# Attention on one core: one packing layout for all heads, odd heads scoring in the array's upper rows, and dense matmuls at the first exps

## The chip, the core and the metric

The kernel runs on one core of a Trainium2 chip. The metric is the device time of the program in microseconds (us). The engines are TensorE (PE; PEld is its weight load), VectorE (DVE), ScalarE (ACT), GpSimd (POOL) and SyncE (SP), which here only issues DMAs. Each has its own instruction queue and runs in order; semaphores join them.

## The reference

The input is x of 1024 tokens by 256 features. It passes through four residual blocks, each behind a layer norm:

```
x = x + attn_a(layernorm(x))     # 16 heads of 16, full softmax over 1024 keys, LoRA on Wq, Wk, Wv, Wo
x = x + ffn(layernorm(x))        # 256 -> 1024, exact gelu, -> 256; both weights ternary
x = x + attn_b(layernorm(x))     # 16 heads of 48 = q, k, v of 16; mixes heads of one token
x = x + ffn(layernorm(x))
```

The change touches `attn_a` alone: per head `softmax(q k^T / 4) v` with 1024 queries and 1024 keys.

## The kernel before

**Setup (0 to about 30 us).** x is normalised and transposed, the LoRA products are merged into the weights, and q and k are projected in eight items (`ITEMS`: q or k, heads 0 to 7 or 8 to 15, first or second half of the tokens). Each projection is cut into an fp16 first part (ACT, `first_part`) and a rest (DVE, `second_part`). A head's q and k then take 64 partition rows: four terms of 16, so that one fp16 matmul over 64 rows gives nearly an fp32 product. Two spare rows of the 64 carry the softmax shift.

**Where the terms lie.** For heads 0 to 7 all four terms are written out (`first_halves`, in the memory of `pbuf`, ACT writing one part twice). For heads 8 to 15 only three are (`last_halves`, in `parts`).

**Packing.** DMAs issued by SP (eight also by POOL) spread a head's terms from 16 partitions to the 64 rows of `k_rows` and `q_rows` (`spread`). For heads 0 to 7 that is one DMA a call, for 8 to 15 two. The upper 64 partitions get the queries again, and, in a separate tensor `k_far` in `parts`, the second half of the keys (`whole_group` repeats them by two DMAs a group). There are four groups of four heads.

**Maximum pass.** A tile of 128 queries against 1024 keys is two matmuls, one in the lower 64 rows (near keys) and one in the upper 64 (far keys), into a pair of PSUM banks (`max_tile`). DVE reduces 1024 columns to the row maximum (`take_max`, L1097). Sixteen tiles make a unit; a unit is a group of four heads and half of the queries, eight units in all (u = 0 to 7). When the sixteen are there, DVE cuts the maxima in two fp16 parts (`cut_max`), PE transposes them (`shift_rows`), ACT copies them to `m_rows`, and SP writes them by a DMA into the spare rows of the queries (`land_shift`).

**Score, exp and PV.** A unit has 32 steps. Step s takes head s % 4 and 128 keys: one score matmul of 64 rows (L1405) into one of three banks, one exp on ACT (L888) into `pbuf`; every fourth step PE multiplies four tiles by v (`times_v`, L1419, fp32, four column groups of 32). In the same loop every second step has a maximum tile of the next unit, and at the end of a unit's steps those of the unit after it begin, so the first seven (`LEAD`) of a unit stand ahead. Before the scores of a unit PE waits for its shift to have landed (`shift_landed`). At the end of a unit ACT copies PV out to `o_un` (`evacuate_pv`, L873), which lies in `parts` too. Unit 7 runs in the tail, whose order on all engines is the hand-written list `TAIL_ORDER`.

**Order on SP around the change.** Groups 0 and 1 are packed early. Then, in the order of the program: shift of unit 0; the 24 spreads and two repeats of group 2; two bias loads; shift of unit 1; the 24 spreads and two repeats of group 3; shift of unit 2; then the later shifts, one a unit. SP stops at each wait, and what stands behind it waits with it.

**Before the loop.** PE does the sixteen maximum tiles of unit 0 with the last two q items and the eight v projections between them, then the seven lead tiles of unit 1, behind the first of which stand the merged Wo (`merged_weight`) and the transposition of unit 0's maxima. At the fourth lead tile it waits for the first shift, and then starts the scores. `keep_clock` issues dense 128x128x512 matmuls; before, only at the start of the program (17).

Of the kernel before, what the change touches and what calls it, by code (L numbers as in the profile page):

```python
# [50 lines left out]
SHIFT_ROWS = (slice(59, 64, 4), slice(61, 64, 2))  # L51
# [21 lines left out]
WARM_UP = 17  # L73
SCORE_BANKS = (4, 5, 7)
# [213 lines left out]
def build(nc, a):  # L288
# [6 lines left out]
    with ExitStack() as ctx:  # L295
# [17 lines left out]
        last_halves = parts[:, 2048:8192].bitcast(F16).rearrange("p (m a t) -> p m a t", m=2, a=TWO + 1)  # L313
        k_far = parts[:, 8192:16384].bitcast(F16).rearrange("p (h t) -> p h t", h=H)
# [6 lines left out]
        far_group = parts[:, 8192:16384].bitcast(F16).rearrange("p (g j t) -> p g j t", g=NG, j=G)  # L321
# [117 lines left out]
        far_keys_packed = sem("far_keys_packed")  # L439
# [70 lines left out]
        def term(c, m, which, v):  # L510

            if c == 0:
                return first_halves[:, m, (0, 1 if m == K_ else 2, 3)[which], v]
            return last_halves[:, m, which, v]

        def first_terms(c, m, v):

            if c == 0:
                return first_halves[:, m, 0:3:2, v] if m == K_ else first_halves[:, m, 0:2, v]
            return last_halves[:, m, 0:1, v]  # L520

        def spread(eng, rows, m, h, v, done):

            c, hh = divmod(h, HC)
            src = slice(HD * hh, HD * hh + HD)
            if c == 0:
                eng.dma_start(rows, first_halves[src, m, :, v]).then_inc(done, 16)
                return
            for i in range(TWO):
                if i == 0:  # L530
                    terms = last_halves[src, m, 0:2, v] if m == K_ else \
                        last_halves[src, m, 0:1, v].broadcast_to([HD, TWO, v.stop - v.start])
                else:
                    terms = last_halves[src, m, 0:3:2, v] if m == K_ else last_halves[src, m, 1:3, v]
                eng.dma_start(rows[ROWS // 2 * i:ROWS // 2 * i + ROWS // 2], terms).then_inc(done, 16)  # L535

        def near_keys(eng, h, v, done):
            spread(eng, k_rows[0:ROWS, h, v], K_, h, v, done)

        def far_keys(eng, h, done):  # L540
            spread(eng, k_far[ROWS:2 * ROWS, h, :], K_, h, slice(HALF, T), done)
# [5 lines left out]
        def group_count(g):  # L547
            return 16 * 3 * G * (1 if g < NG // 2 else TWO)
# [12 lines left out]
        def _(sp):  # L561
# [30 lines left out]
            for j in range(G):  # L592
                near_keys(sp, j, first_half, head_packed[j])
            part_is_cut(sp, K_, 0, 1)
            for j in range(G):
                far_keys(sp, j, head_packed[j])
# [5 lines left out]
            for j in range(G):  # L602
                near_keys(sp, j, second_half, far_keys_packed)
# [3 lines left out]
            def whole_group(g):  # L607
                for h in range(G * g, G * g + G):
                    near_keys(sp, h, whole, group_packed[g])
                    for qh in (0, 1):  # L610
                        queries(sp, h, 0, qh, group_packed[g])
                sp.wait_ge(group_packed[g], group_count(g))
                sp.dma_start(k_far[ROWS:2 * ROWS, G * g:G * g + G, :], k_rows[0:ROWS, G * g:G * g + G, HALF:T]) \
                    .then_inc(group_repeated[g], 16)
# [3 lines left out]
            whole_group(1)  # L618

            def land_shift(g, qh, u):  # L620
# [3 lines left out]
                else:  # L624
# [4 lines left out]
                sp.dma_start(q_rows[SHIFT_ROWS[g // 2], g, qh, :, :].rearrange("o h t -> o (h t)"),  # L629
                             m_rows[0:TWO * n, :]).then_inc(shift_landed, 16)  # L630
# [4 lines left out]
            whole_group(2)  # L635
# [4 lines left out]
            whole_group(3)  # L640
# [124 lines left out]
        def _(act):  # L765
# [39 lines left out]
            def first_part(i):  # L805
# [3 lines left out]
                src = is_filled(act, ("proj", i)).unsqueeze(1).broadcast_to([P, TWO if c == 0 else 1, HALF])  # L809
# [80 lines left out]
            def exp_unit(g, qh, u):  # L890
# [16 lines left out]
            for done in (far_keys_packed, second_half_packed):  # L907
                act.wait_ge(done, 16 * G)
            act.wait_ge(group_packed[1], group_count(1))
            for s in range(G):  # L910
                exp_tile(0, s)
            with act.Fori(0, NG - 1) as g:
                exp_unit(g, 0, g * 2)
                exp_unit(g, 1, g * 2 + 1)

                for n in (2, 3):
                    act.wait_ge(group_packed[n], group_count(n))
# [361 lines left out]
        def _(pe):  # L1279
# [82 lines left out]
            def keep_clock(n):  # L1362
                for _ in range(n):
                    pe.matmul(ps[:, PAIR_BANKS[0], :], onesb[:, 0:P], onesb[:, :], start=True, stop=True)  # L1364

            pe.wait_ge(consts, 4)
            keep_clock(WARM_UP)
# [3 lines left out]
            def max_tile(g, qh, u, k):  # L1371
# [8 lines left out]
                for n, keys in ((0, k_group[0:ROWS, at, j, 0:HALF]), (1, far_group[ROWS:2 * ROWS, at, j, :])):  # L1380
                    q = q_rows[ROWS * n:ROWS * n + ROWS, at, qh, j, P * qt:P * qt + P]
                    ins = pe.matmul(ps[:, b + n, :], q.rearrange("p g t -> p (g t)"), keys.rearrange("p g t -> p (g t)"),  # L1382
                                    start=True, stop=True)
# [14 lines left out]
            def score_tile(g, qh, u, s):  # L1398
# [6 lines left out]
                pe.matmul(ps[:, b, :], k_group[0:ROWS, at, j, P * c:P * c + P].rearrange("p g t -> p (g t)"),  # L1405
# [238 lines left out]
```

## Time and profile before

| | |
|---|---|
| three runs | 352.35, 353.03, 353.84 us; median 353.03 |
| the profiled execution | 353.56 us; span of its instructions 351.7 us, so 1.86 us lie around it |
| busy share of the span | PE 92%, DVE 80%, ACT 69%, POOL 37% |
| chain that ended last | PE 63%, SP's queue 10%, DVE 8%, ACT 7%, POOL 5%, issue 3%, DMA 2% |
| granted TensorE clock, mean | 0.976 of full |

The page cuts the span into 40 slices of 8.8 us and gives busy tenths:

```profile
PE   7999786999979999999999999999998978779796
PEld 3653342222212222222222244338744735447685
DVE  7466999799978999999999543516959997999774
ACT  1575113688858888988888867896479533577694
```

The chain of waits goes back from the last instruction to what released each; the timeline gives instructions in order of time, merged where they follow each other; the idle time before one stands in brackets with the instruction or DMA that ended it. Matmul ends are modelled: a 512-column matmul is recorded with some 0.38 us, while the next one on the same rows starts some 0.22 us after it.

### The profile page before, as it was taken

How to read it: one execution, taken by the hardware profiler on the slowest of the kernel's cores; microseconds unless marked ns; L12 is line 12 of the kernel's file. 1: busy time of each engine (PE TensorE's matmuls, PEld its weight loads, DVE VectorE, ACT ScalarE, POOL GpSimd, SP SyncE). 2: the span in 40 equal slices, each digit the busy share in tenths (PEclk: the TensorE clock that was granted, in tenths of full speed). 3: DMA queues.
4: the chain of work that ended last, by engine and by line, in shares of the span. 5: the costliest groups of instructions: out<-in, count | busy, mean ns of one | idle time of the engine just before them, and what ended most of it. 6: DMA issues, size and time to landing. Idle time of an engine off the chain costs nothing.

```text
span 351.7 us, 5515 instructions
## 1 busy us (share of the span) xinstructions
PE 324.5 (92%) x1909; PEld 146.1 (42%) x1909; DVE 280.6 (80%) x471; ACT 243.5 (69%) x465; POOL 128.5 (37%) x133
## 2 busy tenths in 40 slices
PE   7999786999979999999999999999998978779796
PEld 3653342222212222222222244338744735447685
DVE  7466999799978999999999543516959997999774
ACT  1575113688858888988888867896479533577694
POOL 5042019999200000000006000400499959995030
PEclk9999998799989999999999999999999989999899
DMA  8937862354340000000000000000000000000011
GB/s 223 315 56 141 140 174 38 64 112 88 64 92 0 1 2 1 2 0 3 0 3 1 1 2 1 2 0 2 0 3 0 1 0 2 0 0 2 1 61 60
DMA packets 14814, 14.57 MB, mean 41 GB/s; under 512 B 4995, under 2 KB 13126, under 8 KB 14598
## 3 DMA queue, kind: packets, MB, share of 16 engines
q1 hardware_dynamic: 12358, 12.09, 15.1%
q10 hardware_dynamic: 2176, 1.64, 1.6%
q0 software_dynamic: 256, 0.52, 0.9%
q8 instruction: 15, 0.25, 0.3%
q14 instruction: 9, 0.07, 0.1%
HBM read 5.78 MB, written 1.05 MB: 19 GB/s over the span
## 4 chain that ended last, share of the span: by engine, by line
PE 63%; SPq 10%; DVE 8%; ACT 7%; POOL 5%; issue 3%; DMA 2%; ACTq 0%; DVEq 0%; POOLq 0%
PE ps L1419 14%; PE ps L1405 12%; SPq L535 8%; PE ps L1559 6%; PE ps L1547 6%; PE ps L1382 5%; PE ps L1334 4%; DVE mx L1097 3%; POOL pbuf L750 3%; PE ps L1532 3%; PE ps L1364 2%; PE ps L1591 2%; DMA pack<-m_rows 1%; ACT ps L931 1%; PE ps L1302 1%
## 5 line engine op out<-in xcount | busy, mean ns | idle before, releaser
L1097 DVE TENSOR_REDUCE mx<-ps 128x1 f32<-128x1024 f32 x128 | 150.3, 1219 | 9.8 <-PE ps L1382 8.6
L888 ACT ACTIVATE pbuf<-ps 128x512 f32<-128x512 f32 x256 | 135.7, 600 | 29.7 <-PE ps L1405 28.6
L1405 PE MATMUL ps<-pack 64*128 64x512 f16 x256 | 87.7, 386 | 3.6 <-DMA pack<-m_rows 1.9
L1419 PE MATMUL ps<-pbuf,v_slot 128*32 128x512 f32 x512 | 69.7, 618 | 1.1 <-ACT parts L873 1.1
L1405 PEld LDWEIGHTS ps<-pack 64*128 64x128 f16 x256 | 23.3, 95 | 82.1 <-ACT pbuf L888 48.5
L1382 PE MATMUL ps<-pack 64*128 64x512 f16 x128 | 49.2, 387 | 5.1 <-DVE mx L1097 4.8
L1382 PE MATMUL ps<-parts,pack 64*128 64x512 f16 x128 | 50.2, 399 | 0.0
L750 POOL TENSOR_TENSOR pbuf<-wT 128x1024 f32<-128x1024 f32 (+3 forms) x32 | 48.2, 1538 | 3.4 <-ACT wT L960 3.4
L705 POOL COPY v_slot<-v_sb 128x512 f32<-128x512 f32 x8 | 4.9, 614 | 113.5 <-PE ps L1419 92.0
L681 POOL TENSOR_TENSOR rstd<-rstd,minus_half 128x2 f32<-128x2 f32 x16 | 11.3, 708 | 71.7 <-DVE rstd L1016 71.7
L1191 DVE SCALAR_TENSOR_TENSOR pack<-ps,g_unit,pack 128x512 f16<-128x512 f32 (+1 forms) x40 | 24.6, 639 | 14.2 <-ACT pack L943 14.1
L1547 PE MATMUL ps<-v_sb,w_nat 128*128 128x512 f16 (+1 forms) x160 | 31.0, 337 | 2.7 <-DVE v_sb L1183 2.5
L1559 PE MATMUL ps<-w_nat,pack 128*128 128x256 bf16 x256 | 31.4, 273 | 0.8 <-DVE pack L1191 0.8
L931 ACT ACTIVATE ps<-ps,b_col 128x512 f32<-128x512 f32 (+1 forms) x40 | 23.5, 610 | 8.1 <-PE ps L1547 8.1
L1559 PEld LDWEIGHTS ps<-w_nat,pack 128*128 128x128 f16 x256 | 25.0, 98 | 5.4 <-DVE pack L1191 1.0
L1204 DVE TENSOR_REDUCE s_wide<-pbuf 128x64 f32<-128x1024 f32 (+3 forms) x32 | 25.4, 813 | 2.2 <-POOL pbuf L750 2.0
L943 ACT ACTIVATE pack<-ps,g_unit 128x512 f16<-128x512 f32 (+1 forms) x40 | 23.5, 643 | 0.2
L953 ACT ACTIVATE xn<-x_res,offset,rstd 128x256 f32<-128x256 f32 x24 | 13.1, 595 | 13.8 <-POOL offset L686 13.7
L1547 PEld LDWEIGHTS ps<-v_sb,w_nat 128*128 128x128 f16 x160 | 15.3, 99 | 15.6 <-DVE v_sb L1183 2.8
L1382 PEld LDWEIGHTS ps<-pack 64*128 64x128 f16 x128 | 11.9, 94 | 22.9 <-DVE mx L1097 12.3
L1419 PEld LDWEIGHTS ps<-pbuf,v_slot 128*32 128x32 f32 x512 | 10.4, 108 | 18.8 <-issue 18.1
L733 POOL TENSOR_TENSOR x_res<-x_res,w_nat 128x512 f32<-128x512 f32 x12 | 15.2, 1272 | 2.3 <-ACT xn L953 2.3
(145 smaller groups left out, 392.8 us busy)
## 6 DMA issues: line engine op xcount, KB each, us to landing
w_nat<-in_L_ffn_w_dram SPq DMA_DIRECT2D x2, 1024.0 KB, 6.7
pack<-pack SPq DMA_DIRECT2D x3, 512.0 KB, 4.9
pack<-pbuf SPq DMA_DIRECT2D x20, 64.0 KB, 2.5
x_res<-in_L_attn_a_x_dram SPq DMA_DIRECT2D x4, 256.0 KB, 3.6
pack<-parts SPq DMA_DIRECT2D x16, 64.0 KB, 2.3
pack<-parts SPq DMA_DIRECT2D x32, 32.0 KB, 2.0
out_dram<-x_res SPq DMA_DIRECT2D x4, 256.0 KB, 2.1
w_nat<-in_L_attn_b_Wqkv_dram ACTq DMA_DIRECT2D x1, 768.0 KB, 5.8
```

The source lines that it names most:

```text
L535: eng.dma_start(rows[ROWS // 2 * i:ROWS // 2 * i + ROWS // 2], terms).then_inc(done, 16)
L750: pool.tensor_tensor(out, in0, in1, ALU.mult).then_inc(products, 1)
L888: act.activation(pbuf[:, c % 2, j, :], ps[:, b, :], ACT.Exp, scale=scale_bits).then_inc(drained[b], 1)
L931: act.activation(src, src, ACT.Gelu, bias=b1_col[:, f:f + 1]).then_inc(gelu_ready, 1)
L1097: dve.tensor_reduce(mx[:, par, k:k + 1], ps[:, b:b + 2, :].rearrange("p b k -> p (b k)"), AX_X, ALU.max) \
L1191: dve.scalar_tensor_tensor(out=g_lo[:, kept(r, s), f, 0:width], in0=bank(key)[:, 0:width], scalar=g_unit[:, f:f + 1], in1=g_hi[:, kept(r, ...
L1204: dve.tensor_reduce(s_raw[:, t % 2, i, 0:nj], terms, AX_X, ALU.add).then_inc(reduced, 1)
L1382: ins = pe.matmul(ps[:, b + n, :], q.rearrange("p g t -> p (g t)"), keys.rearrange("p g t -> p (g t)"), start=True, stop=True)
L1405: pe.matmul(ps[:, b, :], k_group[0:ROWS, at, j, P * c:P * c + P].rearrange("p g t -> p (g t)"), q_rows[0:ROWS, at, qh, j, :].rearrange("p ...
L1419: ins = pe.matmul(ps[32 * j:32 * j + 32, PV_BANK, :], v_slot[:, qh, c, j, :], pbuf[:, c % 2, j, :], start=(c == 0), stop=(c == TT - 1))
L1547: ins = pe.matmul(out, w1T[:, c, P * f:P * f + P], x12[:, part, c, v], start=(part == 0 and c == 0), stop=(part == 1 and c == DC - 1))
L1559: ins = pe.matmul(out, part[:, k, f, v], w2T[:, f, :], start=(f == 0 and n == 0 and i == 0), stop=(f == FC - 1 and n == 1 and i == 1))
```

## The change

1. **One layout.** `last_halves` gets four terms like `first_halves`; ACT writes the first part twice for heads 8 to 15 too. `spread` is one DMA for every head. Group 1 takes 8 spreads in place of 12, groups 2 and 3 take 8 each in place of 24.
2. **Keys in both halves.** `k_far` goes; `k_rows` is filled in the upper 64 partitions too, with all 1024 keys. The repeat of a group's keys is 512 KB in place of 256 KB.
3. **Order on SP.** All spreads of groups 2 and 3 come first, then the repeats of 2, the repeats of 3, the bias loads, and then the shift of unit 1. ACT waits for both groups before the first PV copy.
4. **Odd heads.** `score_tile` uses the upper rows for heads 1 and 3 of a group. So the shift is written into both halves: two DMAs a unit.
5. **Dense matmuls.** Three ahead of each of the last two maximum tiles of unit 0, and three ahead of each of the seven lead tiles of unit 1: 27 in all, into the PV bank, the first three behind a wait for that bank's last v copy.

```diff
-        last_halves = parts[:, 2048:8192]...(m=2, a=TWO + 1)
-        k_far = parts[:, 8192:16384]...
+        last_halves = parts[:, 0:8192]...(m=2, a=TWO * TWO)
 def spread(eng, rows, m, h, v, done):
-            if c == 0:
-                eng.dma_start(rows, first_halves[src, m, :, v]).then_inc(done, 16)
-                return
-            for i in range(TWO):
...
-                eng.dma_start(rows[ROWS // 2 * i:ROWS // 2 * i + ROWS // 2], terms).then_inc(done, 16)
+            eng.dma_start(rows, (last_halves if c else first_halves)[HD * hh:HD * hh + HD, m, :, v]).then_inc(done, 16)
+        def both_queries(eng, h, done):
+            g, j = divmod(h, G)
+            spread(eng, q_rows[0:ROWS, g, :, j, :], Q_, h, slice(0, T), done)
 # SP, packing
-                near_keys(sp, j, second_half, far_keys_packed)
+                keys(sp, j, j % 2, second_half if j % 2 == 0 else first_half, score_keys_packed)
+            def spread_group(g):
+                for h in range(G * g, G * g + G):
+                    keys(sp, h, 0, whole, group_packed[g])
+                    both_queries(sp, h, group_packed[g])
+            def repeat_group(g):
+                sp.wait_ge(group_packed[g], GROUP_COUNT)
+                sp.dma_start(k_rows[ROWS:2 * ROWS, <group g>], k_rows[0:ROWS, <group g>]).then_inc(group_repeated[g], 16)
+                sp.dma_start(q_rows[ROWS:2 * ROWS, g], q_rows[0:ROWS, g]).then_inc(group_repeated[g], 16)
 # land_shift
-                sp.dma_start(q_rows[SHIFT_ROWS[g // 2], g, qh, :, :]..., m_rows[0:TWO * n, :])
+                for r in range(TWO):
+                    sp.dma_start(q_rows[slice(ROWS * r + 59, ROWS * r + 64, 4), g, qh, :, :]..., m_rows[0:TWO * n, :])
 # SP, order
             land_shift(0, 0, 0)
-            whole_group(2)
+            spread_group(2)
+            spread_group(3)
+            repeat_group(2)
+            repeat_group(3)
             (two bias loads)
             land_shift(0, 1, 1)
-            whole_group(3)
             land_shift(1, 0, 2)
 # ACT, first_part
-                src = ....broadcast_to([P, TWO if c == 0 else 1, HALF])
+                src = ....broadcast_to([P, TWO, HALF])
 # ACT, exp_unit
+                if qh == 0:
+                    for n in (2, 3):
+                        act.wait_ge(group_packed[n], GROUP_COUNT)
                 evacuate_pv(g, qh, u)
 # PE, score_tile
-                pe.matmul(ps[:, b, :], k_group[0:ROWS, ...], q_rows[0:ROWS, ...])
+                rows = slice(ROWS * (j % 2), ROWS * (j % 2) + ROWS)
+                pe.matmul(ps[:, b, :], k_group[rows, ...], q_rows[rows, ...])
 # PE, before the loop
             for k in range(FILLS):
+                if k >= FILLS - 2:
+                    pe.wait_ge(drained[PV_BANK], base[PV_BANK])
+                    keep_clock(KEEP_UP, PV_BANK)          # KEEP_UP = 3
                 max_tile(0, 0, 0, k)
             for k in range(LEAD):
+                keep_clock(KEEP_UP, PV_BANK)
                 max_tile(0, 1, 1, k)
```

## Rows read from the trace of the kernel before

**Rows 1.** Chain that ended last, stretch 97 to 104 (start, us, what)

```profile
97.98 4.39 DMA pack<-m_rows
103.61 1.86 PE ps L1419 x8
107.43 0.99 PE ps L1419 x8
```

**Rows 2.** Timeline of ACT: shift copy, PV copies, exps (start, us; idle in brackets)

```profile
75.22 0.27 ACT L869 COPY m_rows<-ps 128x128 f16<-128x128 f16 x1 [0.42 <-PE ps L1396]
...
83.54 0.58 ACT L873 COPY parts<-ps 128x512 f32 x1
106.55 0.58 ACT L873 COPY parts<-ps 128x512 f32 x1
126.35 0.58 ACT L873 COPY parts<-ps 128x512 f32 x1
146.06 0.58 ACT L873 COPY parts<-ps 128x512 f32 x1
...
199.78 2.06 ACT L888 ACTIVATE pbuf<-ps 128x512 f32<-128x512 f32 x4 [0.33 <-PE ps L1405]
```

**Rows 3.** Timeline of PE and its weight loads: shift waits, unit 6 without max passes

```profile
80.66 0.11 PEld L1405 LDWEIGHTS ps<-pack 64*128 64x128 f16 x2 [0.52 <-DMA pack<-m_rows]
...
102.42 0.39 PE L1405 MATMUL ps<-pack 64*128 64x512 f16 x1 [1.87 <-DMA pack<-m_rows]
...
199.36 0.82 PE L1405 MATMUL ps<-pack 64*128 64x512 f16 x3
200.43 0.39 PE L1405 MATMUL ps<-pack 64*128 64x512 f16 x1 [0.26 <-ACT pbuf L888]
```

**Rows 4.** Timeline of DVE, maxima of units 0 and 1

```profile
33.93 1.23 DVE L1097 TENSOR_REDUCE mx<-ps 128x1 f32<-128x1024 f32 x1 [0.62 <-PE ps L1382]
...
46.58 5.84 DVE L1097 TENSOR_REDUCE mx<-ps 128x1 f32<-128x1024 f32 x5 [0.28 <-PE ps L1382]
...
54.72 9.14 DVE L1097 TENSOR_REDUCE mx<-ps 128x1 f32<-128x1024 f32 x8 [0.54 <-PE ps L1382]
65.71 8.44 DVE L1097 TENSOR_REDUCE mx<-ps 128x1 f32<-128x1024 f32 x7 [1.85 <-PE ps L1382]
```

**Rows 5.** Windows: engines' busy us (instructions), granted clock, DMA share, GB/s

```profile
35.00:40.00 5.00, 3.83 (x18) 1.82 (x16) 4.96 (x7) 0.75 (x2) 0.00 (x0) 1.00 0.89 148
...
61.00:66.00 5.00, 5.00 (x22) 1.07 (x20) 3.15 (x4) 2.34 (x5) 4.67 (x4) 0.54 0.34 62
...
75.00:80.00 5.00, 5.00 (x33) 1.32 (x33) 5.00 (x5) 4.30 (x9) 4.72 (x4) 1.00 0.87 203
```

**Rows 6.** Timeline, all engines, 49 to 50: maximum tile 14, last v copy

```profile
49.64 0.39 PE L1382 MATMUL ps<-pack 64*128 64x512 f16 x1
49.74 0.37 ACT L816 COPY v_sb<-ps 128x256 f32<-128x256 f32 x1 [1.22 <-PE ps L1352]
```

**Rows 7.** Timeline of SP's queue, 34 to 98

```profile
34.09 8.22 SPq L527 DMA_DIRECT2D pack<-pbuf  x12
...
55.92 16.75 SPq L535 DMA_DIRECT2D pack<-parts  x24
...
78.27 0.73 SPq L629 DMA_DIRECT2D pack<-m_rows  x1
...
97.32 0.61 SPq L615 DMA_DIRECT2D pack<-pack  x1
```

**Rows 8.** Lines by form: first parts on ACT (busy, mean ns)

```profile
L810 ACT ACTIVATE pbuf<-ps,kq_scaled 128x1024 f16<-128x1024 f32 x4 | 4.5, 1116 | 1.3 <-PE ps L1334 1.2
L810 ACT ACTIVATE parts<-ps,kq_scaled 128x512 f16<-128x512 f32 x4 | 2.7, 684 | 2.7 <-PE ps L1334 2.7
```

**Rows 9.** Chain that ended last, stretch 206 to 236

```profile
208.43 0.54 PE ps L1405 x2
...
229.68 0.54 PE ps L1405 x2
```

More of the change, by code:

```diff
@@ L50 @@
 ROWS = TWO * TWO * HD
-SHIFT_ROWS = (slice(59, 64, 4), slice(61, 64, 2))
+SHIFT_ROWS = slice(59, 64, 4)
 DROPPED = HD - TWO
@@ L73 @@
 WARM_UP = 17
+KEEP_UP = 3
 SCORE_BANKS = (4, 5, 7)
@@ L628, in land_shift @@
                 n = G * TT // 2
-                sp.dma_start(q_rows[SHIFT_ROWS[g // 2], g, qh, :, :].rearrange("o h t -> o (h t)"),
-                             m_rows[0:TWO * n, :]).then_inc(shift_landed, 16)
+                for r in range(TWO):
+                    sp.dma_start(q_rows[slice(ROWS * r + SHIFT_ROWS.start, ROWS * r + SHIFT_ROWS.stop, SHIFT_ROWS.step), g, qh, :, :]
+                                 .rearrange("o h t -> o (h t)"), m_rows[0:TWO * n, :]).then_inc(shift_landed, 16)
             land_shift(0, 0, 0)
@@ L808, in first_part @@
                 out = first_terms(c, m, slice(HALF * s, HALF * s + HALF))
-                src = is_filled(act, ("proj", i)).unsqueeze(1).broadcast_to([P, TWO if c == 0 else 1, HALF])
+                src = is_filled(act, ("proj", i)).unsqueeze(1).broadcast_to([P, TWO, HALF])
                 act.activation(out, src, ACT.Identity,
@@ L906, in _ @@
                 act.wait_ge(head_packed_by_pool[j], 32)
-            for done in (far_keys_packed, second_half_packed):
+            for done in (score_keys_packed, second_half_packed):
                 act.wait_ge(done, 16 * G)
-            act.wait_ge(group_packed[1], group_count(1))
+            act.wait_ge(group_packed[1], GROUP_COUNT)
             for s in range(G):
@@ L1379, in max_tile @@
                     pe.wait_ge(drained[b], base[b] + u * (FILLS // 2) + k // 2)
-                for n, keys in ((0, k_group[0:ROWS, at, j, 0:HALF]), (1, far_group[ROWS:2 * ROWS, at, j, :])):
-                    q = q_rows[ROWS * n:ROWS * n + ROWS, at, qh, j, P * qt:P * qt + P]
-                    ins = pe.matmul(ps[:, b + n, :], q.rearrange("p g t -> p (g t)"), keys.rearrange("p g t -> p (g t)"),
+                for n in (0, 1):
+                    rows = slice(ROWS * n, ROWS * n + ROWS)
+                    ins = pe.matmul(ps[:, b + n, :], q_rows[rows, at, qh, j, P * qt:P * qt + P].rearrange("p g t -> p (g t)"),
+                                    k_group[rows, at, j, HALF * n:HALF * n + HALF].rearrange("p g t -> p (g t)"),
                                     start=True, stop=True)
@@ L1404, in score_tile @@
                 at = bass.ds(g, 1)
-                pe.matmul(ps[:, b, :], k_group[0:ROWS, at, j, P * c:P * c + P].rearrange("p g t -> p (g t)"),
-                          q_rows[0:ROWS, at, qh, j, :].rearrange("p g t -> p (g t)"), start=True, stop=True) \
+                rows = slice(ROWS * (j % 2), ROWS * (j % 2) + ROWS)
+                pe.matmul(ps[:, b, :], k_group[rows, at, j, P * c:P * c + P].rearrange("p g t -> p (g t)"),
+                          q_rows[rows, at, qh, j, :].rearrange("p g t -> p (g t)"), start=True, stop=True) \
                     .then_inc(filled[b], 1)
```

64 lines of the change are left out of this document (22 added, 42 removed).

## The prediction

> **What bounds the kernel now.** I read the page's chain of waits first: SP's queue holds 10% of it and a DMA 2%, although SP computes nothing. In order of time the chain runs from the first shift through SP's issues up to the DMA that writes the shift of unit 2: it is issued at 97.98 and lands 4.39 us later [rows 1]. PE stands 1.87 us before the scores of unit 2 [rows 3], and the next PV group takes 1.86 us in place of 0.99, for the clock has fallen [rows 1]. The PV copies on ACT price the whole: they lie 23.01 us apart over this unit (83.54 to 106.55), then 19.80 and 19.71 [rows 2]. One stall costs 3.3 us against 19.71.
>
> Then the other dip of the clock. From 61 to 66 the granted clock is 0.54, most of it at the lower of its two levels, 1.2 GHz [rows 5]. DVE, elsewhere without a pause, stands 1.85 us there waiting for a maximum tile [rows 4]. The cut of unit 1's maxima, behind the seven that end at 74.15, depends on that run.
>
> Third, the loop. A group of four steps takes 2.39 us (exps of unit 6 start at 199.78 and at 202.17, four exps 2.06 and 0.33 idle before them [rows 2]). I looked at unit 6 behind its last maximum tile, since there PE has only scores and PV: it idles 0.26 us for a bank that ACT must free, and the pace is the same [rows 3]. So the loop is a circle of latencies: last exp of four, score, PV, next score, its exp. PE's load is not what sets it. DVE is nearly as long: a maximum takes 1.14 to 1.21 us (9.14/8, 5.84/5, 8.44/7 [rows 4]; I use 1.18), and two fall in a group of four steps: 2.36.
>
> **The shift of unit 2 (gain).** With the spreads of group 3 moved ahead, SP has nothing but two small DMAs between the shift of unit 1 and that of unit 2, a unit later. The stall goes: 3.3 us [rows 2]. What is late next is the shift of unit 1.
>
> **The shift of unit 1 (cost).** Before, SP issued it at 78.27, behind 24 spreads (16.75 us, 0.70 each with the holds), two repeats and the biases [rows 7], and PE waited 0.52 us until 80.66 [rows 3], so it is wanted at 80.14. After:
> - The spreads began at 55.92 [rows 7]; now 1.1 later (see the dense matmuls) and one more DMA of the first shift, 0.7: 57.7.
> - 16 spreads x 0.70 = 11.2 us of issuing, to 68.9. They carry 16 x 128 KB = 2.1 MB. The nearest stretch, the packing of group 1, moved 148 GB/s at share 0.89 [rows 5], 166 GB/s at share 1: 12.6 us. With some 1.4 from issue to flow, from 59.1 to 71.7. The transfers end after the issues.
> - Four repeats of 512 KB, 2.1 MB: 203 GB/s at 0.87 in the stretch of the same repeats before [rows 5], 233 GB/s at share 1: 9.0 us, to 80.7. SP issues those of group 3 when all spreads have landed, near 72, the biases by 75; 0.26 MB more, 1.1 us, to 81.8.
> - The shift itself is ready at 75.5 (75.22 + 0.27 [rows 2]), as before. Its DMA lands behind what was issued ahead: in the trace that of 97.98 took 4.39 us [rows 1] with a 512 KB repeat issued at 97.32 ahead of it [rows 7], that of 78.27 at most 2.4. So it lands near 82.0, 1.8 us after it is wanted. With some of the clock's fall behind it (the stall of unit 2 cost 3.3 us with a wait of 2.4 after PE's last other work, so 0.9 more than it), and the 0.5 that was paid here before, I take +2.0.
>
> Bounds: if the transfers keep up with SP's issues, the shift lands at 75.5 + 0.7 + 2.4 = 78.6, in time: -0.3. At 128 GB/s for all 4.4 MB (1 MB issued in 8.22 us, 12 DMAs [rows 7]) it lands at 93.5: +13. I take the middle rows, since they are the same kinds of transfer at high load.
>
> The Trainium skill (DMA: Bandwidth & Descriptors, "Queues, rings and completion order") states that each DMA engine takes the descriptors of a ring in ring order. That speaks against this change: a small DMA can't pass 2 MB of repeats on SP's row. The 4.39 us above agree. Were it not so, the shift would land at about 78.6, in time, and the sum would be 2.0 lower.
>
> **Dense matmuls (cost and gain, net 0).** PE reached maximum tile 14 at 49.64; now it first waits for the last v copy, 49.74 + 0.37 = 50.11 [rows 6], then three matmuls of 0.22 each (spacing of scores back to back: 0.82 for three less 0.39, halved [rows 3]), to 50.8. DVE wants that tile at about 50.1 (46.58 plus three of 1.17 [rows 4]), gets it at 51.2: +1.1. The merged Wo, the transposition and the first shift move by the same 1.1. The second lead tile then has three more matmuls before it: +0.7. So DVE's run that began at 54.72 begins at about 56.5. From there three matmuls and a tile, 0.66 + 0.22, fit below 1.17 a maximum. If the clock stays at 2.4 GHz, the pause of 1.85 us [rows 4] goes, and the fifteen maxima end at 56.5 + 15 x 1.18 = 74.2, against 65.71 + 8.44 = 74.15. Net 0. If the clock falls in spite of them, +1.8; if the first delay is partly hidden, -0.5. The exps start 1.7 us later than before, but the shift copy, not they, ends the unit's first part.
>
> **Odd heads in the upper rows.** In a group of four steps PE has four scores and two near tiles on the lower rows, six slots of 0.22. Now it is four and four, so four slots, 0.43 less. By the circle above that is worth 0 in units 0 to 6: the score that ACT waits for comes first behind PV in both kernels. In the tail it is another matter. From 206 to 232 the chain is PE alone, and seven times two or three scores stand next to each other (first, one of the threes, and the last in [rows 9]); in each, one score now runs beside its neighbour. 7 x 0.22 = 1.5 us. Bounds 0 (ACT's exps take over) and -1.5; I take -0.9, since ACT idled at most of these places.
>
> The Trainium skill (TensorEngine Tiling (Array Packing), "The Solution") promises up to twice the rate for contractions of at most 64 rows, and 8 groups x 0.43 would be 3.4 us a unit by it; the same page ("PSUM Bottleneck") says that emptying PSUM may then bound. The row of unit 6 agrees with the second.
>
> **What costs nothing, and its cover.** Four first parts become 1116 ns instead of 684 [rows 8], 1.7 us of ACT; ACT idles 2.7 us ahead of these four, waiting for PE [rows 8], and 1.2 ahead of a v copy [rows 6]. The one that DVE waits for delays the first maximum by 0.4, and DVE later waited 0.62 for PE anyway [rows 4]. Without the cover: +0.4. ACT's wait for groups 2 and 3 before the first PV copy: packed by 71.5 to 75, wanted at 83.54 [rows 2]. The repeat of group 1 grows by 256 KB and is wanted only at the first scores, some 8 us after it. The second shift DMA, 0.7 of issue: a shift is ready 4.6 us before it is wanted (75.5 and 80.14), and two DMAs with a landing of 2.4 take 3.8.
>
> **Sum.** -3.3 + 2.0 + 0 - 0.9 = -2.2 us. On the profiled execution: span 351.7 to 349.5, time 353.56 to 351.4. The median of the runs was 0.53 below the profiled one, so 350.8.
>
> **Rivals.**
> 1. The shift of unit 1 is in time: -3.3 - 0.9 = -4.2, 348.8. For it: the DMA share was often only 0.3 to 0.6 in that stretch, the engines have room. Against: 4.4 MB in 23 us.
> 2. The other side: the shift of unit 1 is held up by repeats and spreads far longer than unit 2's was. A landing at L costs L - 80.1 + 0.9 for the clock - 0.5 paid before; it decides from 83.9, where that is 4.2, the other two gains together. At 86 it is 6.3: 353.0 - 3.3 + 6.3 - 0.9 = 355.1. For it: 166 GB/s is a stretch at share 0.89, near full. Against: nothing else uses the DMAs then.
> 3. The dense matmuls delay, and the clock falls all the same, since PE still waits for the first shift among them: +1.8, 352.6. Against: three matmuls a maximum make PE busy 75% of that stretch in place of 20%.
> 4. The loop was bound by PE after all, and now goes at DVE's pace: 16 x 1.18 + 0.45 = 19.3 against 19.71, -0.4 in each of six units, 348.5 in all. For it: DVE's 2.36 and PE's load lie close under 2.39 and can't be told apart from it by their busy shares. Against: unit 6.
> 5. With less to do PE's clock falls inside the loop. It is busy 1.85 of 2.39 us then, as in unit 6's second half before, and no dip shows there. At 1.2 GHz PE would need 3.7 us a group, 1.3 more than now; three groups are 4 us, 355.
>
> **Chances.** Forecast 0.42, rival 1 0.20, rival 2 0.14, rival 3 0.13, rival 4 0.08, rival 5 0.03. What a measurement of this kernel can tell from no change is 0.5%, 1.8 us: below 351.3 is faster, above 354.8 slower. Faster: two thirds of the forecast, nearly all of 1 and 4: 0.53. Slower: most of 2, some of 3, and 5: 0.16. The rest 0.31. The range of 348.2 to 354.6 leaves out the far ends of 2 and 5 and the case that 1 and 4 come together.
>
> **What would show it.** PV copies: the second 21 to 22 us behind the first, the third 19.8 behind that; a wait on `pack<-m_rows` near 80 and none near 100. DVE's run of maxima without a pause from about 56.5, granted clock 1.0 from 57 to 70, the last of fifteen ending near 74.2. The group of four at 2.39 still. The tail from 206 to 234 shorter by 1 us. The prediction is wrong if the loop's pace changes, if the first PV copy moves by over 1.5 us, or if the shift of unit 1 lands before 80 or after 84.

## The result and the profile after

The changed kernel is slower, by 0.9%. Its eleven runs have a median of 356.20 us (354.43 to 356.88); eleven runs of the kernel before beside them 353.69 us (350.29 to 359.36). The ratio is 1.0093, 95% interval 1.0065 to 1.0122. A ratio leaves out the runs of either kernel that lie over 1.5% above its fastest, at a lower granted clock, so it isn't the ratio of the medians. The profiled execution took 356.88 us, span 355.1 against 351.7: 3.4 us more.

The page of the changed kernel, parts 1 and 4 (busy us and share; chain that ended last by engine):

```profile
PE 324.3 (91%) x1934; PEld 141.8 (40%) x1936; DVE 281.8 (79%) x471; ACT 243.9 (69%) x465; POOL 128.6 (36%) x133
...
PE 70%; DVE 15%; ACT 7%; issue 3%; POOL 2%; SPq 1%; DMA 1%; ACTq 0%; DVEq 0%; POOLq 0%
```

SP's queue has gone from 10% of the chain to 1%. That share alone would have promised a gain. What is left of it is short and expensive. First ACT's timeline of the changed kernel, the line that answers to [rows 2] (start, duration; idle before it in brackets):

```profile
76.61 0.27 ACT L860 COPY m_rows<-ps 128x128 f16<-128x128 f16 x1 [0.52 <-PE ps L1389]
...
87.21 1.57 ACT L879 ACTIVATE pbuf<-ps 128x512 f32<-128x512 f32 x3 [4.77 <-PE ps L1399]
...
90.66 0.58 ACT L864 COPY parts<-ps 128x512 f32 x1
...
110.35 0.58 ACT L864 COPY parts<-ps 128x512 f32 x1
...
209.66 0.58 ACT L864 COPY parts<-ps 128x512 f32<-128x512 f32 x1
...
236.15 0.59 ACT L864 COPY parts<-ps 128x512 f32<-128x512 f32 x1
```

The PV copies and the shift copies are fixed marks: the same instruction in both kernels. Set against those before (75.22, 83.54, 106.55 [rows 2]; 206.06 and 234.04 for the last two), they give an account of the 3.4 us without a gap (a unit's PV copy stands behind the wait for the next unit's shift):

| stretch | before | after | difference |
|---|---|---|---|
| start to the shift copy of unit 1 | 75.22 | 76.61 | +1.4 |
| to the first PV copy (late shift of unit 1) | 8.32 | 14.05 | +5.7 |
| to the second (late shift of unit 2 before) | 23.01 | 19.69 | -3.3 |
| five more units | 99.51 | 99.31 | -0.2 |
| unit 7, to its PV copy | 27.98 | 26.49 | -1.5 |
| from there to the end of the span | 117.7 | 119.0 | +1.3 |

SP's queue of the changed kernel, the lines that answer to [rows 7]:

```profile
56.78 1.51 SPq L618 DMA_DIRECT2D pack<-m_rows  x2
58.41 14.09 SPq L521 DMA_DIRECT2D pack<-parts  x16
72.55 0.60 SPq L600 DMA_DIRECT2D pack<-pack  x1
73.19 0.76 SPq L602 DMA_DIRECT2D pack<-pack  x1
75.42 0.85 SPq L600 DMA_DIRECT2D pack<-pack  x1
76.32 2.29 SPq L602 DMA_DIRECT2D pack<-pack  x1
78.67 2.33 SPq L630 DMA_DIRECT2D w_nat<-in_L_ffn_b_dram  x1
81.05 2.24 SPq L630 DMA_DIRECT2D w_nat<-in_L_attn_b_bout_dram  x1
```

The shift was ready at 76.9. SP reached it at 83.33. An issue takes 0.6 us when the queue is free; here three in a row take 2.2 to 2.3 each, the first of them the last repeat itself. In the kernel before, one took 2.04 us at 76.18 with at most 0.9 MB issued and not landed (256, 512 and 128 KB, since the spreads had landed). Then the chain of waits that ended last in the changed kernel, which answers to [rows 1]:

```profile
83.33 0.71 SPq L618
84.04 0.04 issue
84.08 2.36 DMA pack<-m_rows
```

And PE's timeline of the changed kernel at the same place, which answers to [rows 3]:

```profile
86.48 0.61 PE L1399 MATMUL ps<-pack 64*128 64x512 f16 x2 [4.46 <-DMA pack<-m_rows]
...
87.87 1.93 PE L1413 MATMUL ps<-pbuf,v_slot 128*32 128x512 f32 x8
```

PE stood 4.46 us, and the PV group behind it took 1.93 us: the clock had fallen, as after the stall of unit 2 before [rows 1]. PE came to that wait at 82.02.

DVE's timeline of the changed kernel, its run of maxima, the answer to [rows 4]:

```profile
46.72 3.49 DVE L1089 TENSOR_REDUCE mx<-ps 128x1 f32<-128x1024 f32 x3 [0.28 <-PE ps L1374]
51.49 2.35 DVE L1089 TENSOR_REDUCE mx<-ps 128x1 f32<-128x1024 f32 x2 [1.28 <-PE ps L1374]
...
57.14 3.49 DVE L1089 TENSOR_REDUCE mx<-ps 128x1 f32<-128x1024 f32 x3 [1.54 <-PE ps L1374]
61.05 14.43 DVE L1089 TENSOR_REDUCE mx<-ps 128x1 f32<-128x1024 f32 x12 [0.42 <-PE ps L1374]
```

The pause of 1.85 us is gone, as forecast: the granted clock is 1.00 from 57 to 65. In its place are 1.28, 1.54 (0.54 before) and 0.42: 2.7 us for 1.85. The fifteen maxima themselves took 17.9 us (3.49 + 14.43) in place of 17.6. So the run ends at 75.48 in place of 74.15; 0.14 of that was there at 46.72 (46.58 before [rows 4]).

### The profile page after: what moved, and what is told of

Its sections match the earlier page's. It is cut to its first block, busy times and chain, and to the rows that moved or that the text cites. A ratio compares the mean times of both kernels' runs of the same rounds, so it can differ in the third digit from the quotient of the medians.

```text
span 355.1 us, 5540 instructions
## 1 busy us (share of the span) xinstructions
PE 324.3 (91%) x1934; PEld 141.8 (40%) x1936; DVE 281.8 (79%) x471; ACT 243.9 (69%) x465; POOL 128.6 (36%) x133
## 4 chain that ended last, share of the span: by engine, by line
PE 70%; DVE 15%; ACT 7%; issue 3%; POOL 2%; SPq 1%; DMA 1%; ACTq 0%; DVEq 0%; POOLq 0%
PE ps L1413 16%; PE ps L1399 13%; PE ps L1374 7%; DVE mx L1089 6%; PE ps L1557 6%; PE ps L1545 6%; PE ps L1326 4%; PE ps L1356 4%; PE ps L1530 3%; PE ps L1589 2%; ACT ps L923 1%; PE ps L1344 1%; PE ps L1294 1%; ACT parts L864 1%; DVE s_wide L1196 1%
## 5 line engine op out<-in xcount | busy, mean ns | idle before, releaser
L1413 PE MATMUL ps<-pbuf,v_slot 128*32 128x512 f32 x512 | 68.9, 611 | 1.3 <-ACT parts L864 1.3
L1399 PEld LDWEIGHTS ps<-pack 64*128 64x128 f16 x256 | 18.8, 94 | 80.9 <-ACT pbuf L879 52.4
L1374 PEld LDWEIGHTS ps<-pack 64*128 64x128 f16 x256 | 13.2, 93 | 28.7 <-DVE mx L1089 21.4
L1589 PE MATMUL ps<-w_nat,xT 128*128 128x512 f32 x32 | 17.7, 679 | 0.0
```

Of the source, the lines that this page charges most:

```text
L1374: ins = pe.matmul(ps[:, b + n, :], q_rows[rows, at, qh, j, P * qt:P * qt + P].rearrange("p g t -> p (g t)"), k_group[rows, at, j, HALF * n ...
L1399: pe.matmul(ps[:, b, :], k_group[rows, at, j, P * c:P * c + P].rearrange("p g t -> p (g t)"), q_rows[rows, at, qh, j, :].rearrange("p g t ...
L1413: ins = pe.matmul(ps[32 * j:32 * j + 32, PV_BANK, :], v_slot[:, qh, c, j, :], pbuf[:, c % 2, j, :], start=(c == 0), stop=(c == TT - 1))
L1589: ins = pe.matmul(out, xT[:, d, P * t:P * t + P], wqkv[:, d, :].rearrange("p (h n) -> p h n", h=H)[:, :, 0:2 * HD], start=False, stop=(d = ...
```

## The experiments

Ten kernels ran. All but one edit the changed kernel; "reordered kernel" is the first of them. The last column is the granted clock from the last PV copy to the end of the span. Times are medians of the runs; the ratio is to the kernel before, run beside them (its medians were 353.0 to 354.3 us, single runs 349.6 to 359.8).

| kernel | median us | ratio, 95% interval | span | first PV copy | last PV copy to end | clock there |
|---|---|---|---|---|---|---|
| shift_before_repeat3 | 350.53 | 0.9919 (0.9884 to 0.9954) | 349.0 | 84.02 | 119.5 | 0.93 |
| biases_behind_shift | 355.63 | 1.0091 (1.0057 to 1.0126) | 354.8 | 90.36 | 119.0 | 0.96 |
| no_dense | 355.34 | 1.0048 (1.0002 to 1.0094) | 353.9 | 88.49 | 119.9 | 0.93 |
| scores_low | 357.83 | 1.0132 (1.0069 to 1.0195) | 358.5 | 91.05 | 117.7 | 0.97 |
| before_repeats_behind | 350.75 | 0.9921 (0.9892 to 0.9951) | 349.7 | 84.74 | 117.8 | 0.97 |
| shift_first_no_dense | 350.37 | 0.9915 (0.9871 to 0.9958) | 346.2 | 83.37 | 117.4 | 0.97 |
| late_dense | 348.51 | 0.9876 (0.9832 to 0.9921) | 347.1 | 82.14 | 119.5 | 0.93 |
| tail_dense | 350.27 | 0.9924 (0.9894 to 0.9955) | 349.8 | 84.91 | 119.4 | 0.97 |
| second_by_act | 348.23 | 0.9890 (0.9851 to 0.9928) | 347.7 | 82.67 | 119.6 | 0.93 |
| order_low | 352.79 | 1.0014 (0.9981 to 1.0046) | 351.3 | 84.55 | 119.6 | 0.93 |

Each kernel has one trace. DVE's run of maxima that begins near 46 (46.58 in the kernel before [rows 4], 46.72 in the changed one) begins anywhere from 45.98 to 47.14 in the ten traces. I call its start the common mark; what the dense matmuls do is read as a distance from it.

### The order on SP's queue: shift_before_repeat3

```diff
             repeat_group(2)
+            land_shift(0, 1, 1)
             repeat_group(3)
             (two bias loads)
-            land_shift(0, 1, 1)
             land_shift(1, 0, 2)
```

> The changed kernel with one edit: SP issues the shift of unit 1 behind the repeats of group 2 and ahead of the repeats of group 3 and the biases. Theory (the shift of unit 1 is late because four repeats and two bias loads stand before it): it is issued at about 76.9, lands by 81, the ACT pause of 4.77 us before the fourth-last exps of unit 0 goes or is under 1 us, the first PV copy comes at about 85 in place of 90.66, the total falls by 5 to 5.7 us, to a span near 349.8 and a ratio to the kernel before of 0.990 to 0.998. Rival (the transfers of the spreads and of group 2 alone, 3.1 MB, are what delays it): it still lands at 83 or later, the total falls by less than 3 us. Second rival: the repeats of group 3, issued later, now delay the shift of unit 2 (wanted near 101): a pause there of over 1 us.

SP's queue of the reordered kernel:

```profile
72.62 0.79 SPq L602 DMA_DIRECT2D pack<-pack  x1
76.20 1.97 SPq L618 DMA_DIRECT2D pack<-m_rows  x2
```

The shift goes out as soon as it is ready, at 76.20, and no wait on it is left at either unit. From the shift copy of unit 1 to the first PV copy it takes 8.11 us (14.05 in the changed kernel, 8.32 before). The span is 6.1 us shorter than the changed kernel's, the median 5.7. The first rival falls: the spreads and group 2's repeats do not make the shift late. The second falls too: the second PV copy comes 19.69 us after the first. So the whole of the +5.7 is the place of one instruction behind two repeats and two bias loads.

### How the queue delays it: biases_behind_shift

```diff
             repeat_group(2)
             repeat_group(3)
-            (two bias loads)
             land_shift(0, 1, 1)
+            (two bias loads)
             land_shift(1, 0, 2)
```

> The changed kernel with one edit: the two bias loads stand behind the shift of unit 1, the four repeats still ahead of it. Tells apart how the shift is delayed. Theory A (SP's issues themselves are held while much is outstanding, the transfers then follow quickly): without the two held issues of 2.33 and 2.24 us the shift is issued at 78.7, and as the next issue may be held in their place, by 81; it lands 2.4 us after its last issue, 82.5 to 84; total 2.5 to 4 us less than the changed kernel. Theory B (only the bytes ahead on the queue count): 0.26 MB of 2.4 MB less, some 1.3 us earlier, total 1 to 1.5 us less.

SP's queue of this kernel:

```profile
76.87 2.43 SPq L602 DMA_DIRECT2D pack<-pack  x1
79.36 4.26 SPq L618 DMA_DIRECT2D pack<-m_rows  x2
```

The shift stands behind the repeats at 79.36, 4 us earlier, and its two tiny DMAs now take 4.26 us to issue. PE's wait goes from 4.5 to 3.7 us, the median from 356.20 to 355.63 (the span, 355.1 to 354.8, began with a shift copy 0.4 later). So whoever stands behind the four repeats pays, first as a held issue: the hold passes to the next DMA, and the bias loads were not its cause. Theory B is nearer (forecast 1.0 to 1.5 us, measured 0.8 in the wait and 0.6 in the median, both below it). Theory A fails in its number, though the held issues it started from are real. Whether bytes or the number of transfers set the hold, no run tells.

### The stall of the kernel before, alone: before_repeats_behind

The kernel before with the shift of unit 2 ahead of group 3's two repeats:

```diff
-            whole_group(3)
-            land_shift(1, 0, 2)
+            spread_whole(3)
+            land_shift(1, 0, 2)
+            repeat_whole(3)
```

> The kernel before with one edit: SP issues the shift of unit 2 ahead of the two repeats of group 3 in place of behind them. Theory (the stall of unit 2 is the order on SP's queue alone): the shift is issued at about 95.5 and lands by 98, PE's wait of 1.87 us and the slow clock behind it go, the second PV copy comes at 103.3 in place of 106.55, the total falls by 3.3 us (span 348.4, ratio 0.988 to 0.994). Rival (24 spreads before it still hold it up): it lands at 100 or later, gain under 1.5 us.

ACT's timeline of this kernel, the first two PV copies:

```profile
84.74 0.58 ACT L878 COPY parts<-ps 128x512 f32 x1
...
104.45 0.58 ACT L878 COPY parts<-ps 128x512 f32 x1
```

19.71 us between them, against 23.01: the stall is worth 3.3 us and was this order alone. The span falls by 2.0 and not 3.3, because the start was unlucky in this trace: the shift copy of unit 1 came at 76.62 in place of 75.22, behind a longer stretch at the slow clock (about 57 to 67, against 59 to 66). The ratio is 0.9921.

### The dense matmuls: no_dense, shift_first_no_dense, late_dense

`no_dense` takes all 27 away from the changed kernel, `shift_first_no_dense` from the reordered one:

```diff
-                if k >= FILLS - 2:
-                    pe.wait_ge(drained[PV_BANK], base[PV_BANK])
-                    keep_clock(KEEP_UP, PV_BANK)
                 max_tile(0, 0, 0, k)
...
-                keep_clock(KEEP_UP, PV_BANK)
                 max_tile(0, 1, 1, k)
```

> The changed kernel without its 27 dense matmuls before the loop and the wait ahead of them. Theory (they cost DVE two pauses, 1.28 and 1.54 less what was there before, and give back only the 1.85 of the slow clock, net +1.4 on the shift copy of unit 1, 76.61 against 75.22): the clock falls again near 59 to 65, the shift copy returns to about 75.2, everything on SP comes some 1.5 us earlier, the total is 1.2 to 1.6 us less than the changed kernel. Rival (they pay): the clock falls longer or the cut comes later, the total is the same or larger.

> The reordered kernel (shift of unit 1 ahead of group 3's repeats) without the 27 dense matmuls. Theory (they are a net loss of 1.35 us at the shift copy of unit 1, as seen with the late shift in place): first PV copy at 82.7 in place of 84.02, span 347.6 against 349.0, the clock low for some us near 60. Rival (without the late shift to hide behind, the slow clock costs more): copy at 84 or later.

`late_dense` keeps, in the reordered kernel, only those ahead of the third to seventh lead tile (`k` from 2 to 6); the three ahead of each of the last two tiles of unit 0 go too:

```diff
+                if k == 2:
+                    pe.wait_ge(drained[PV_BANK], base[PV_BANK])
+                if k >= 2:
+                    keep_clock(KEEP_UP, PV_BANK)
                 max_tile(0, 1, 1, k)
```

> The reordered kernel with dense matmuls only ahead of the third to seventh lead tile of unit 1 (15 in place of 27, none where DVE waits for a tile). Theory (the loss comes from the twelve that stand where DVE has nothing left to do): DVE's pauses of 1.28 and 1.0 go, its run starts at 54.7; if the clock then stays at 2.4 GHz the shift copy of unit 1 comes near 73.6 and the span is near 346.7. Rival (the clock had fallen because PE did little from 50 on, and fifteen later ones come too late): the clock still falls near 59, the shift copy stays at 75 or later, span 347.6 to 349.

The clock tells them apart. Windows of no_dense (first fence) and of the changed kernel (second; busy us of PE, PEld, DVE, ACT, POOL; the third number from the end is the granted clock):

```profile
57.00:60.00 3.00, 1.81 (x7) 0.40 (x7) 2.42 (x4) 1.38 (x3) 2.81 (x3) 0.66 0.60 70
60.00:65.00 5.00, 4.67 (x18) 0.66 (x18) 4.60 (x5) 2.52 (x5) 4.72 (x4) 0.52 0.77 154
```

```profile
57.00:60.00 3.00, 2.69 (x14) 0.82 (x13) 2.86 (x3) 0.00 (x0) 2.82 (x3) 1.00 0.12 20
60.00:65.00 5.00, 4.17 (x23) 1.07 (x23) 4.45 (x5) 2.95 (x6) 4.72 (x4) 1.00 0.82 134
```

Without them the clock goes to its lower level, 1.2 GHz, and still the shift copy of unit 1 comes earlier: 75.26 against 76.61. In the reordered kernel it comes at 75.25 against 75.91, but there the common mark lay 0.7 apart. From that mark the shift copy comes 29.9 us later in all six traces with the 27 (29.89 to 29.94) and 28.6 later in the two without (28.60, 28.61): 27 dense matmuls hold the clock and lose 1.3 us there.

Of the whole time less is seen. no_dense's median is 0.9 below the changed kernel's (forecast 1.2 to 1.6), and those of the reordered kernel with and without them (350.53, 350.37) don't differ. shift_first_no_dense has its first PV copy at 83.37 (forecast 82.7), and its span, 346.2, owes 2.1 us to a short last part. Its runs spread from 347.4 to 351.9 us at granted clocks of 0.956 to 0.980, the reordered kernel's from 348.1 to 351.3 at 0.976 to 0.995. So in some executions the 27 may give back what they cost here. The one trace that hints at it is before_repeats_behind: with the clock low until 67 its shift copy came 29.9 us from the mark, as late as with the 27.

DVE's timeline of late_dense:

```profile
46.09 5.84 DVE L1089 TENSOR_REDUCE mx<-ps 128x1 f32<-128x1024 f32 x5 [0.28 <-PE ps L1374]
...
54.23 3.49 DVE L1089 TENSOR_REDUCE mx<-ps 128x1 f32<-128x1024 f32 x3 [0.54 <-PE ps L1374]
58.79 14.42 DVE L1089 TENSOR_REDUCE mx<-ps 128x1 f32<-128x1024 f32 x12 [1.07 <-PE ps L1374]
```

With fifteen, none of them where DVE waits for PE, the clock is 1.00 through 52 to 67, the pause of 1.28 is gone and that of 1.54 is 0.54, as in the kernel before. The shift copy comes at 74.03 (forecast 73.6), 27.9 us from the common mark: 2.0 less than with the 27, 0.7 less than with none. The median falls from 350.53 to 348.51 (six runs, beside another set of runs of the kernel before; the intervals of the two ratios overlap). shift_first_no_dense, run in the same set, has 350.37. The mechanism was right and the place was wrong: twelve of the 27 stood where DVE had nothing left in its banks.

### The second shift DMA: second_by_act

In `late_dense` a pause of 1.07 us is left, where PE waits for the first shift. ACT issues the upper half:

```diff
-                for r in range(TWO):
+                for r in range(1 if isinstance(u, int) and u == 0 else TWO):
                     sp.dma_start(q_rows[...], m_rows[0:TWO * n, :]).then_inc(shift_landed, 16)
# ACT
             copy_shift(0)
+            is_drained(act, ("shift",))
+            act.dma_start(q_rows[<upper rows 59 and 63>, 0, 0, :, :]..., m_rows[0:G * TT, :]).then_inc(shift_landed, 16)
```

> The kernel with fifteen late dense matmuls (shift of unit 1 ahead of group 3's repeats), and ACT in place of SP issues the upper-half copy of the first shift, so that both copies go out at once. Theory (the second shift DMA was not free: at the first scores it stands 0.7 us behind the first, and DVE pauses 1.07 us there because PE waits for it): the pause of 1.07 falls to about 0.4, the shift copy of unit 1 comes at 73.4 in place of 74.03, span 346.4 to 346.6 in place of 347.1. Rival (DVE's pause is the dense matmuls or the scores' place in PE's order, not the landing): no change of the pause, span 347.

DVE's timeline of it:

```profile
59.04 14.43 DVE L1092 TENSOR_REDUCE mx<-ps 128x1 f32<-128x1024 f32 x12 [0.61 <-PE ps L1377]
```

The pause falls by 0.46, so the landing of the second DMA is part of its cause; the 0.61 that is left has none shown. The shift copy came at 74.56, not at the 73.4 of the forecast; from the common mark it comes 0.2 earlier than in late_dense. The total doesn't show it (348.23 and 348.51).

### The upper rows: scores_low, order_low

Both put every score on the lower rows again, in the changed and in the reordered kernel:

```diff
-                rows = slice(ROWS * (j % 2), ROWS * (j % 2) + ROWS)
+                rows = slice(0, ROWS)
...
-                keys(sp, j, j % 2, second_half if j % 2 == 0 else first_half, score_keys_packed)
+                keys(sp, j, 0, second_half, score_keys_packed)
```

> The changed kernel with all scores in the lower rows again (keys and shift still in both halves; the second half of the odd heads' keys of group 0 goes to the lower rows). Theory (the upper rows are worth nothing in the loop and 1.5 us in the tail): unit pace 19.7 in both, the stretch from the last PV copy of the loop to the FFN's first y parts 1.5 us longer than in the changed kernel; total 0 to 1.5 us more, since the changed kernel gave 1.3 us back later. Rival (the loop gains too): the unit pace rises to over 19.8.

> The reordered kernel (shift of unit 1 ahead of group 3's repeats, 27 dense matmuls) with all scores in the lower rows. No stall disturbs it, so it prices the upper rows alone. Theory: unit pace 19.71 in place of 19.69, 0.15 us over the loop; from the PV copy of unit 6 to that of unit 7 it takes 28.0 in place of 26.5 us; from there to the end 117.7 to 117.8 as in the two kernels with lower-row scores, in place of 119.5: span 349.0, no difference. Rival (the later loss has nothing to do with the upper rows, it is the phase of the slow clock): the last part takes 119 to 119.5 and the span is 350.5.

Undisturbed, the loop's unit takes 19.71 us with lower rows and 19.69 with both: 0.02, nothing. Unit 7 takes 27.98 against 26.49, so the tail's gain is 1.5 us. order_low lasts to 351.3, the reordered kernel to 349.0; medians 352.79 and 350.53. Of those 2.3, 0.5 lie ahead of the first PV copy (setup), 0.2 in the loop, 1.5 in unit 7, 0.1 behind it. Here my theory of order_low failed and its rival held: the last part took 119.6 us with lower rows too. So the tail's gain is real and stays, and the 1.3 us lost later are not its doing.

scores_low has something more in its trace. PE's timeline behind the stall:

```profile
88.05 1.93 PE L1413 MATMUL ps<-pbuf,v_slot 128*32 128x512 f32 x8
...
92.58 1.93 PE L1413 MATMUL ps<-pbuf,v_slot 128*32 128x512 f32 x8
...
96.78 1.07 PE L1413 MATMUL ps<-pbuf,v_slot 128*32 128x512 f32 x8
```

4.5 us a group of four steps at the lower clock, for two groups. With both rows in use, in the changed kernel, the next PV group came 3.5 us after the first (87.87 and 91.39), and at full clock. The unit behind the stall took 22.3 us with lower rows, 19.7 with both. That the rows did this is not shown. The two groups did not run at one clock: it came back near 90 in the changed kernel and near 96 in scores_low. In the kernel before, whose scores are all on the lower rows, it was back after one group too, behind a wait of 1.87 us in place of 4.3, and that group took 3.8 us (103.61 and 107.43 [rows 1]). And the profiled execution of scores_low, 360.34 us, is the slowest of only four; its median lies 1.6 us above the changed kernel's, which the 1.5 of unit 7 cover.

### The last part: tail_dense

Between 276 and 310 us every trace has one or two stretches of some microseconds at the lower clock, not at the same place in all. In the kernel before it lay at 284 to 288, in the changed one at 294 to 302 (windows; the first fence is the kernel before, the second the changed one):

```profile
284.00:288.00 4.00, 3.76 (x10) 2.32 (x11) 3.82 (x10) 1.44 (x4) 2.86 (x4) 0.57 0.00 0
```

```profile
294.00:298.00 4.00, 2.67 (x6) 1.18 (x7) 3.83 (x9) 1.68 (x4) 2.98 (x4) 0.57 0.00 0
298.00:302.00 4.00, 4.00 (x9) 2.15 (x8) 2.46 (x9) 0.63 (x2) 2.30 (x3) 0.57 0.00 0
```

`tail_dense` puts 14 dense matmuls into the reordered kernel, where PE waits:

```diff
+            dense = {("lnt", 2, 2): 8, ("bo_y", 1): 6}
             for e in events:
+                if e in dense:
+                    to_fill(pe, e)
+                    keep_clock(dense[e], uses[e][0])
```

> The reordered kernel with 14 dense matmuls in the tail, in two places where PE waits: 8 ahead of the third layer-norm transposition of the third block, 6 ahead of its second output projection, each into the bank that is filled next. Theory (the 1.3 to 1.9 us by which the kernels with upper-row scores lose their tail gain again is PE's slow clock near 283 to 291): granted clock 1.0 there, span 347.2 to 347.7 in place of 349.0. Rival (that stretch is bound by DVE and POOL, the clock only goes with it): span 349 or more.

Windows of tail_dense over the same part:

```profile
280.00:290.00 10.00, 7.00 (x28) 3.31 (x26) 9.46 (x26) 3.48 (x9) 8.06 (x8) 1.00 0.00 0
290.00:300.00 10.00, 9.71 (x35) 5.33 (x35) 9.73 (x24) 3.71 (x8) 7.51 (x10) 1.00 0.00 0
300.00:310.00 10.00, 6.98 (x32) 3.95 (x30) 8.86 (x19) 6.83 (x12) 10.00 (x7) 0.84 0.01 2
```

The clock holds up to 300, falls once behind it, and the last part still takes 119.4 us. The theory fails in this form. Its rival, that DVE and POOL bound this stretch, forecast the span of 349 or more that came, and DVE is busy 95 to 97% of the two windows. But the last column of the table speaks for the clock. Windows from the last PV copy to the end: the kernel before, the changed kernel, shift_first_no_dense, late_dense:

```profile
234.04:351.70 117.66, 103.08 (x622) 70.64 (x620) 94.17 (x222) 75.56 (x145) 68.96 (x62) 0.97 0.03 10
236.15:355.10 118.95, 104.45 (x622) 70.56 (x620) 95.20 (x222) 75.59 (x145) 69.06 (x62) 0.96 0.03 10
228.81:346.20 117.39, 102.56 (x622) 69.17 (x620) 95.17 (x222) 75.63 (x145) 68.99 (x62) 0.97 0.03 10
227.59:347.10 119.51, 106.51 (x622) 71.93 (x620) 94.30 (x222) 75.60 (x145) 68.94 (x62) 0.93 0.03 10
```

Of the twelve traces, four have a granted clock of 0.97 there and no added matmuls, and take 117.4 to 117.8 us; two have 0.96 and take 119.0; five have 0.93 and take 119.5 to 119.9. The score layout doesn't sort them: at 0.97 three have all scores on the lower rows and one has not, at 0.93 one has and four have not. So this part, of the same instructions, goes with how long the clock is low in it, and the +1.3 of the account is of that kind. The same is seen in whole runs of one kernel: second_by_act took 346.21 us at a mean clock of 0.995 and 349.5 to 349.6 at 0.975. tail_dense alone has 0.97 and 119.4: PE was given 14 more matmuls, at 0.22 each an estimated 3.1 us, and they may have cost what they gave. What stays open is why the clock falls in one place or another, and whether a kernel decides it: there is one trace of each.

## Why the prediction was wrong

The forecast was 350.8 us, range 348.2 to 354.6; it became 356.2. The step that failed is **the shift of unit 1**, put at +2.0 and measured at +5.7. The mechanism was right and is shown by shift_before_repeat3: the shift waits behind what SP issued ahead. In the span the forecast was 5.6 short: 3.7 here, 1.4 in the dense matmuls, 1.3 in the last part, less 0.6 and 0.2 that the tail and the loop gave more. The size of the step was off in four terms:

- The spreads. Forecast 166 GB/s, all landed near 72; measured 75.4, when SP could issue group 3's repeats, 2.1 MB in 15.6 us from 59.8: 134 GB/s. The lower bound, 128, was almost met. I had scaled a stretch at DMA share 0.89 up to share 1, and share 1 was not reached: from 60 to 70 it was 0.81. SP took 0.88 us a spread (14.09 for 16) where I had 0.70. Whether the issues held the transfers up or the transfers the issues, no run tells.
- The repeats and biases. Forecast 233 GB/s, scaled up in the same way from 203 at 0.87. The windows of the changed kernel show 208 GB/s from 76 to 82 at share 1.00. Here the share was reached and the rate did not follow.
- The shift's own way. I let it land with the last byte ahead of it, at 82.0. SP could not even issue it until 83.33, and the second of the two DMAs landed 2.36 us after its issue at 84.08, so 86.44. The issue was held, and its way of 2.36 us came on top; the row of 4.39 us [rows 1] could not show this, since there the issue was not held.
- The slow clock behind it. Forecast +0.9, from a wait of 2.4 us; but [rows 3] has PE idle for 1.87, which leaves 1.4 of the 3.3. Measured 1.5: the stretch is 5.94 us longer than in the reordered kernel, and the wait was 4.46.

(The terms as written, 1.8 + 0.9 - 0.5, make 2.2; I had taken 2.0.) This was rival 2, named with its price (a landing at 86 gives 355.1) and given 0.14; the landing came at 86.44. That the price fits so well is in part luck: by its formula 86.44 costs 6.7 us, but PE wanted the shift at 82.02 and not at 80.14, since its own work came later. The rival should have had more weight: 4.4 MB stood in 23 us ahead of one small DMA.

Step by step for the rest:

- **Shift of unit 2**, -3.3: measured -3.3, and before_repeats_behind shows it alone.
- **Dense matmuls**, net 0: +1.4, of which 1.3 is shown to be theirs. The clock held and the 1.85 us came back, as forecast, so rival 3 falls. The two delays were 1.28 and 1.0 (forecast 1.1 and 0.7), the maxima took 0.3 longer in all, and I missed the 0.42 where PE waits for the first shift; I had said that the second shift DMA costs nothing for the later units and counted its 0.7 only on SP. second_by_act shows that in late_dense 0.46 of it stood in DVE's way at the first.
- **Odd heads**: 0 in the loop, -0.9 in the tail; measured -0.04 a unit and -1.5, the far bound. Rivals 4 and 5 fall: the clock is 1.00 in the loop, and the pace is still 2.39 us a group (196.03 to 198.42 in ACT's timeline of the changed kernel):

```profile
196.03 2.06 ACT L879 ACTIVATE pbuf<-ps 128x512 f32<-128x512 f32 x4 [0.33 <-PE ps L1399]
198.42 2.06 ACT L879 ACTIVATE pbuf<-ps 128x512 f32<-128x512 f32 x4 [0.33 <-PE ps L1399]
```

  The page TensorEngine Tiling (Array Packing) of the Trainium skill says two things: up to twice the rate ("Theoretical Speedup") and the emptying of PSUM as a possible bound ("PSUM Bottleneck"). The loop agrees with the second, with 0.02 us a unit gained; the tail, with 1.5 us where PE is the chain, goes some way with the first.
- **Costs at nothing**: behind the longer first parts DVE's run at the common mark began 0.14 later, less than traces differ; ACT's wait for groups 2 and 3 doesn't appear.
- **The last part**, not in the sum at all: +1.3 in this trace. It goes with a granted clock of 0.96 there in place of 0.97; why the clock fell longer is open.

The rule on ring order (the Trainium skill, DMA: Bandwidth & Descriptors, "Queues, rings and completion order") agrees with what is seen: in the changed kernel the shift landed at 86.44, in biases_behind_shift, where it was issued 4 us earlier, PE could go on at 86.14 and no sooner.

**The best version** is the changed kernel with two repairs, the shift ahead of group 3's repeats and fifteen dense matmuls in place of 27: 348.51 us, ratio 0.9876 (0.9832 to 0.9921), from six runs. It beats both kernels.

## What to carry to other kernels

When transfers are merged and moved forward, look at which small transfer now stands behind them on the queue, and when it is wanted. Put it ahead of bulk that nobody needs yet. A filler that keeps PE's clock up belongs where PE waits for a slower engine that still has work, never ahead of the instruction for which that engine waits. And don't scale a rate that was read at a busy share of 0.9 up to share 1: here one kind of transfer never reached that share, and the other reached it without the rate. Last, when two kernels have one trace each, compare the granted clock of each part before a difference of 1 or 2 us is given to the edit.

## What the runs showed of the hardware

- SP's DMA issues, 0.6 us each otherwise, took 2.2 to 2.4 us behind three or four repeats of 512 KB on its queue; two DMAs of 8 KB then took 4.26 us to issue. One issue of 2.04 us came with at most 0.9 MB ahead (kernel before, 76.18).
- Spreads of 128 KB, issued one every 0.88 us, moved 134 GB/s at a DMA share of 0.81; the repeats, whole rows of 8 KB, 208 at 1.00, half again as fast.
- Scores in both halves of the rows gave nothing where PE was not the bound (19.69 us a unit against 19.71) and 1.5 us where PE was the chain (26.49 against 27.98).
- The part from the last PV copy to the end, the same instructions in eleven kernels, took 117.4 to 117.8 us at a granted clock of 0.97 and 119.5 to 119.9 at 0.93.
